# An expert stage re-cut from 24 tiles of two 64-token blocks to 31 tiles of one 128-token block

## The reference

```
normed = (x * rsqrt(mean(x*x) + 1e-6)) * ln_w
probs = softmax(normed @ w_router)              # 16 experts
expert_idx = argmax(probs)
keep = onehot * (cumsum(onehot, axis=1) <= 64)  # at most 64 tokens of a sequence for one expert
h = relu(expert_in @ wi[e])                     # 192 -> 768
expert_out = h @ wo[e]                          # 768 -> 192
next = where(routed, combined, normed)
return x + max(probs) * next
```

## Time and profile before

| | us |
|---|---|
| median of 3 runs | 405.36 |
| lowest, highest | 401.0, 406.44 |
| the profiled execution, whole | 408.49 |
| its span, first to last instruction | 406.8 |
| PE busy in the span | 320.6 (79%) |
| DVE busy | 262.2 (64%) |
| POOL busy | 203.8 (50%) |
| ACT busy | 191.6 (47%) |

### The profile page before, as it was taken

One profiled execution on the slowest core, in us unless ns is written; L12 is line 12 of the kernel. 1 busy time (PEld: TensorE's weight loads), 2 busy tenths in 40 slices (PEclk: granted clock), 3 DMA queues, 4 the chain that ended last, 5 costly groups with the idle time before them and its releaser, 6 DMA issues.

```text
span 406.8 us, 9205 instructions
## 1 busy us (share of the span) xinstructions
PE 320.6 (79%) x3246; PEld 234.4 (58%) x3246; DVE 262.2 (64%) x743; ACT 191.6 (47%) x405; POOL 203.8 (50%) x250
## 2 busy tenths in 40 slices
PE   0058798989889888998987803389999999999990
PEld 0056657769677676977867602345556666555560
DVE  7467846887878788767485636846656565556620
ACT  0613644967768687763844612033333333333320
POOL 5767650552553626401001446577666666755420
PEclk9999967998989899896998965599999999999997
DMA  5328820126152352703208951139311221111100
GB/s 138 89 63 222 244 60 1 21 60 176 33 161 72 96 146 48 203 1 99 75 9 246 291 154 39 39 105 293 107 46 51 60 58 54 48 46 53 48 3 0
DMA packets 33589, 38.22 MB, mean 94 GB/s; under 512 B 6480, under 2 KB 30777, under 8 KB 33556
## 3 DMA queue, kind: packets, MB, share of 16 engines
q1 hardware_dynamic: 25940, 24.58, 21.3%
q0 software_dynamic: 7040, 12.63, 12.5%
q10 hardware_dynamic: 576, 0.59, 0.4%
HBM read 31.36 MB, written 7.21 MB: 95 GB/s over the span
## 4 chain that ended last, share of the span: by engine, by line
PE 58%; POOL 11%; ACT 10%; issue 8%; DVE 7%; DMA 3%; POOLq 0%; ACTq 0%; SPq 0%; DVEq 0%
PE psum L1363 11%; PE psum L1140 7%; PE psum L1342 7%; PE psum L1141 7%; POOL weights L396 6%; PE psum L1347 4%; PE psum L1354 3%; PE psum L1258 3%; ACT shared L574 3%; PE psum L1175 3%; PE psum L1210 2%; POOL blk_token L458 2%; ACT L574 2%; PE psum L1134 2%; DMA token_rows<-shared 2%
## 5 line engine op out<-in xcount | busy, mean ns | idle before, releaser
L1087 DVE COPY shared<-weights 128x1152 f32 x96 | 69.1, 763 | 10.6 <-issue 10.5
L1258 PE MATMUL psum<-ident 128*128 128x128 f32 x200 | 34.0, 334 | 38.1 <-DMA qk_norm<-in_qk_norm 24.5
L473 POOL DMA_INDIRECT tower_out<-shared,oidx x24 | 37.1, 1547 | 38.6 <-DVE shared L1101 38.0
L1258 PEld LDWEIGHTS psum<-ident 128*128 128x128 f32 x200 | 32.6, 247 | 39.2 <-issue 24.5
L1363 PE MATMUL psum<-shared 128*64 128x192 f32 x576 | 52.1, 330 | 0.9 <-ACT shared L672 0.9
L404 POOL TENSOR_TENSOR small<-small,eps_of 128x2 f32<-128x2 f32 x32 | 6.8, 212 | 89.7 <-DVE small L768 66.2
L1363 PEld LDWEIGHTS psum<-shared 128*64 128x64 f32 x576 | 39.2, 137 | 19.4 <-issue 13.8
L1101 DVE SCALAR_TENSOR_TENSOR shared<-psum,shared 128x192 f32<-128x192 f32 x24 | 10.0, 418 | 46.0 <-PE psum L1363 46.0
L1140 PE MATMUL psum<-shared,weights 96*128 96x192 f32 (+1 forms) x96 | 36.2, 464 | 0.8 <-ACT weights L527 0.7
L1342 PE MATMUL psum<-shared 128*64 128x384 f32 x192 | 36.3, 499 | 0.5 <-ACT shared L664 0.5
L668 ACT ACTIVATE shared<-psum 128x768 f32<-128x768 f32 x24 | 19.5, 811 | 36.4 <-PE psum L1347 36.4
(11 more groups left out here) (179 smaller groups left out, 704.2 us busy)
## 6 DMA issues: line engine op xcount, KB each, us to landing
weights<-in_wo SPq DMA_DIRECT2D x16, 576.0 KB, 7.2
weights<-in_wi SPq DMA_DIRECT2D x32, 192.0 KB, 5.2
weights<-in_wi SPq DMA_DIRECT2D x32, 96.0 KB, 5.5
token_rows<-shared SPq DMA_DIRECT2D x14, 192.5 KB, 2.8
tower_out<-shared SPq DMA_DIRECT2D x14, 96.0 KB, 2.3
vectors<-in_vectors SPq DMA_DIRECT2D x1, 672.0 KB, 4.7
token_rows<-shared ACTq DMA_DIRECT2D x2, 192.5 KB, 2.8
blk_token<-expert_lists,blk_entry POOLq DMA_INDIRECT x24, 2.7
```

Source lines behind the costliest of these rows:

```text
L473: G.indirect_dma_start(out=out, out_offset=bass.IndirectOffsetOnAxis(ap=oidx[q % 2][:, :], axis=0), in_=res[q % 2], in_offset=None, bounds ...
L1087: V.tensor_copy(w_now[q % 2][k][:, lo:hi], weights[:, bass.ds(at[k] + lo, hi - lo)]).then_inc(sem(("wi_now", "wo_now")[part]), 1)
L1258: T.matmul(dst, ident[:, :], ident[:, 0:width], start=True, stop=True)
```

## The change

`BT` becomes 128. A block is now a whole tile of one expert, so each product of a tile is made once, for 128 tokens. 2,048 tokens over 16 experts need, beside the first block of each expert, at most 15 further blocks: 16 + 15 = 31 tiles. The first 16 tiles are fixed: tile q is the first block of expert q, PE reads its weights where they lie (`w_of`) and its tokens are column q of the list table. The other 15 are planned as before, with one `w_now` buffer each for odd and even. The whole list table, 64 KB, is read into `list_sb` by one transfer of SP once all lists are written; DVE then copies the column that a planned tile needs (`take_tokens`). `grow` has six buffers, and five tiles are gathered ahead.

```diff
-BT = P // 2
+BT = P
...
-NBLK = NSEQ * P // BT + NE
-NTILE = NBLK // 2
+NLATE = NSEQ * P // BT - 1
+NTILE = NE + NLATE
+NGROW = 6
...
+        def tokens_of(q):
+            return list_sb[:, q:q + 1] if q < NE else blk_token[:, q - NE:q - NE + 1]
...
-            sp.wait_ge(sem("p_logit"), NSEQ)
+            sp.wait_ge(sem("listed"), 16 * NSEQ)
+            load("lists_read", list_sb, lists.rearrange("(p q) o -> p (q o)", p=P))
             for u in range(3):
                 sp.wait_ge(sem(f"rows{u}"), 16)
...
-            list_tile(0)
-            list_tile(1)
             pool.wait_ge(sem("out_plain"), 32 * (NSEQ - 2))
             pool.wait_ge(sem("rows_last"), 32)
-            gather_rows(0)
-            list_tile(2)
-            gather_rows(1)
-            list_tile(3)
-            gather_rows(2)
-            for q in range(4, 8):
-                list_tile(q)
+            pool.wait_ge(sem("lists_read"), 16)
+            for q in range(NGROW - 1):
+                gather_rows(q)
             pool.wait_ge(sem("out_last"), 32)
             for q in range(NTILE):
-                if q + 3 < NTILE:
-                    gather_rows(q + 3)
-                if q + 8 < NTILE:
-                    list_tile(q + 8)
+                if q + NGROW - 1 < NTILE:
+                    gather_rows(q + NGROW - 1)
                 scatter(q)
...
+            unrouted(NPAIR - 1)
             steps = [0]
...
+            def take_tokens(j):
+                dve.wait_ge(sem("lists_read"), 16)
+                col = dve.value_load(blk_list[0:1, j:j + 1], min_val=0, max_val=NLISTS - 1)
+                V.tensor_copy(blk_token[:, j:j + 1], list_sb[:, bass.ds(col, 1)]).then_inc(sem("blk_token"), 1)
...
             for q in range(NTILE):
-                if q + 1 < NTILE:
-                    at = columns(q + 1)
-                    take_weights(q + 1, 0)
+                late_next = NE <= q + 1 < NTILE
+                if late_next:
...
+                    at = dve.value_load(blk_col[0:1, q + 1 - NE:q + 2 - NE], min_val=0, max_val=(NE - 1) * WCOL)
+                    take_weights(q + 1, 0)
                 if q >= 1:
                     result(q - 1)
-                if q + 1 < NTILE:
+                if late_next:
                     take_weights(q + 1, 1)
+                if 1 <= q <= NLATE:
+                    take_tokens(q - 1)
...
+            def w_of(q):
+                return w_by_expert[:, q, :] if q < NE else w_now[q % 2]
...
                 for b in range(2):
-                    for k in range(2):
-                        T.matmul(hid_ps[k * BT:(k + 1) * BT, b, :], gT[:, b * P + k * BT:b * P + (k + 1) * BT],
-                                 w_now[q % 2][k][:, b * WI2:(b + 1) * WI2], start=True, stop=False)
+                    T.matmul(hid_ps[:, b, :], gT[:, b * P:(b + 1) * P], w[:, b * WI2:(b + 1) * WI2], start=True, stop=False)
                 for b in range(2):
-                    for k in range(2):
-                        at = (1 - b) * P + k * BT
-                        last = T.matmul(hid_ps[k * BT:(k + 1) * BT, b, :], gT[REST[b], at:at + BT],
-                                        w_now[q % 2][k][REST[b], FF:WI_COLS], start=False, stop=True)
+                    last = T.matmul(hid_ps[:, b, :], gT[REST[b], (1 - b) * P:(2 - b) * P], w[REST[b], FF:WI_COLS],
+                                    start=False, stop=True)
...
                 for c in range(FC):
-                    for k in range(2):
-                        last = T.matmul(psum[q % 2][k * BT:(k + 1) * BT, 3, 0:D], hidT[:, c * P + k * BT:c * P + (k + 1) * BT],
-                                        w_now[q % 2][k][:, WI_COLS + c * D:WI_COLS + (c + 1) * D], start=c == 0, stop=c == FC - 1)
+                    last = T.matmul(psum[q % 2][:, 3, 0:D], hidT[:, c * P:(c + 1) * P],
+                                    w[:, WI_COLS + c * D:WI_COLS + (c + 1) * D], start=c == 0, stop=c == FC - 1)
```

More of the change, by code:

```diff
@@ L450, in _, with gather_rows @@
             phase_a(pool, 4, turn_pair)
-            pool.wait_ge(sem("listed"), 16 * NSEQ)
-            def list_tile(q):
-                pool.wait_ge(sem("blk_entry"), 1)
+            def gather_rows(q):
+                if q >= NE:
+                    pool.wait_ge(sem("blk_token"), q - NE + 1)
                 G.indirect_dma_start(
[L459 to L469, removed]
+                    out=grow[q % NGROW], out_offset=None, in_=rows,
+                    in_offset=bass.IndirectOffsetOnAxis(ap=tokens_of(q), axis=0),
+                ).then_inc(sem(f"rows{q % NGROW}"), 16)
             def scatter(q):
@@ L734, in _ @@
             dve.wait_ge(sem("ident"), 7)
[L735 to L738, removed]
             def reduce_args(i):
@@ L1047, in _, with total_over @@
             dve.wait_ge(sem("total"), len(BATCHES))
-            dve.wait_ge(sem("halves"), 3)
-            big, big2 = (shared[:, 4608 + 512 * k:4608 + 512 * k + NTILE * NE].rearrange("p (j e) -> p j e", e=NE) for k in range(2))
+            def total_over(v):
+                return v.unsqueeze(1).broadcast_to([P, NLATE, NE])
+            V.tensor_scalar(blk_pen[:, 0:NE], total[:, :], token_iota[:, 0:1], BIG, ALU.is_le, ALU.mult).then_inc(sem("first_pen"), 1)
             nb, cum, ones = (cols(plan, a, NE) for a in (16, 32, 48))
[L1052 to L1056, removed]
+            nth, ej, before, within, length, late = (cols(plan, 112 + 32 * a, NLATE) for a in range(6))
             planned(V.memset(ones, 1.0))
-            planned(V.scalar_tensor_tensor(over_k, total[:, :].unsqueeze(2).broadcast_to([P, NE, SPLIT]), BT + 0.5,
-                                           list_edge[:, :].unsqueeze(1).broadcast_to([P, NE, SPLIT]), ALU.add, ALU.is_gt))
+            planned(V.tensor_tensor(over_k, total[:, :].unsqueeze(2).broadcast_to([P, NE, SPLIT]),
+                                    list_edge[:, :].unsqueeze(1).broadcast_to([P, NE, SPLIT]), ALU.is_gt))
             planned(V.tensor_reduce(nb, over_k, AX, ALU.add))
@@ L1075, in _ @@
-            planned(V.tensor_scalar(late, half_pos[:, 0:1].broadcast_to([P, NTILE]), float(NLISTS), None, ALU.mult))
-            V.tensor_tensor(blk_entry[:, :], length, late, ALU.add).then_inc(sem("blk_entry"), 1)
-            unrouted(NPAIR - 1)
-            def take_weights(q, part):
-                lo, hi = ((0, WI_COLS), (WI_COLS, WCOL))[part]
-                if q >= 2:
-                    dve.wait_ge(sem(("b_hid", "b_y")[part]), q - 1)
-                for e in range(max(2 * q, ARENA_FIRST), min(2 * q + 2, NE)):
-                    dve.wait_ge(sem(f"weights{e}"), 80)
-                for k in range(2):
-                    V.tensor_copy(w_now[q % 2][k][:, lo:hi], weights[:, bass.ds(at[k] + lo, hi - lo)]).then_inc(
-                        sem(("wi_now", "wo_now")[part]), 1)
@@ L1104, in _ @@
-            dve.wait_ge(sem("blk_entry"), 1)
-            dve.wait_ge(sem("weights"), 80 * ARENA_FIRST)
-            at = columns(0)
-            take_weights(0, 0)
-            planned(V.tensor_tensor(big, over(expert_iota[:, :]), ej.unsqueeze(2).broadcast_to([P, NTILE, NE]), ALU.is_equal))
-            planned(V.tensor_tensor(big2, big, over(total[:, :]), ALU.mult))
+            planned(V.tensor_tensor(big, total_over(expert_iota[:, :]), ej.unsqueeze(2).broadcast_to([P, NLATE, NE]), ALU.is_equal))
```

104 lines of the change are left out of this document (62 added, 42 removed).

## The result

The changed kernel takes 441.03 us (median of 4 runs, 437.18 to 443.56) where the kernel before took 403.92 (4 runs, 401.0 to 406.44): 1.0895 times as long, 95% interval 1.0816 to 1.0973. Forecast was 433.5, range 426 to 441; the median lies at the very end of that range, 0.03 us past it. The direction and the mechanism are as forecast; the rise of 37.1 us is 9 us larger than the forecast 28.2. The profiled executions differ by 34.0 us in span: 440.8 against 406.8. The profiled execution of before (408.49) lies above all its timed runs, so this pair shows 3 us less than the medians do.

The account below looks back on a forecast made before the run. PE was taken to bound the expert stage: 29 steps of 5.08 us for 22 of 5.37 gave plus 28.8 us, the beginning minus 0.6, together 28.2 on the median 405.36. Forecast 433.5 us, range 426 to 441.

Parts of the forecast that it names:

- What bounds the kernel, and what a product costs: Expert stage: PE is the bound; a full-height product costs 0.32 us against 0.35 for a half-height pair, so little is saved.
- The rival by which the price goes with the records: Expert stage: twelve output records would take 1.05 us, POOL's 3.4 us a tile would rule, total 381 us; chance 3%.
- The two 64-row products side by side: Left-over products at L1341 overlap and take 0.65 us; rival without overlap: 1.30 us, total 453.5; chance 6%.
- a step of up to 5.3: Expert stage: case where shape changes all stay, PE's step 5.3 us a tile and the total 440 us.
- a first gather near 260.6: Start of expert stage: sign of being right, first gather at 260.6 where it stood at 261.17, a gain of 0.6 us.
- a first hidden product within 2 us of 266: Start of expert stage: sign of being right, PE's first hidden product within 2 us of 266 in the timeline.
- the signs for being wrong: Step below 4.8 or above 5.3 us, PE waiting for DVE or a gather in the last 15 tiles, first tile after 268.
- PE's step: Each tile: transposes 0.88, hidden 1.30, left-over 0.65, output 1.95, two shape changes 0.30, together 5.08 us for 5.37.
- The beginning: Before the first gather: plan and two list fetches go, a 64 KB read comes; minus 0.6 us, ends minus 3.4 and plus 2.3.
- The late tiles: Last 15 tiles run without waits; rival stall of 1.5 us a tile, plus 22 us, 455; chance 3%.
- the 0.4 us of longer steps near the start: Early expert stage: 0.4 us above 22 x 5.37 in the kernel before, forecast to stay after the change.
- 0.3 off the last tile for two changes of shape: Last hidden product to the end: 8.3 us before, forecast 8.0 with two changes of shape fewer.

Follow-up runs that it names:

- e2: Kernel before with the products of every tile's second block left out: step 5.35 us for 5.37, one timed execution 404.19 us.
- e6: Changed kernel with the left-over channels' products (64 rows by 128 columns) left out, result wrong: step 4.19 us, one timed execution 421.07 us.
- e9: Changed kernel with the left-over product ahead of the main hidden product: step 5.157 us as median of all tiles, one timed execution 437.79 us.
- e4: Kernel before with the left-over product ahead of the main hidden product: step 5.22 us, 402.05 against 406.12 us, ratio 0.9941.
- e1: Changed kernel with its last seven tiles (24 to 30) left out: 402.84 us against 406.12 for the kernel before, ratio 0.986.
- e3: Changed kernel with each full-height product issued as two half-height ones with the same weights: step 5.37 us, one run 440.81 us.
- e5: Changed kernel with PE's filler begun when the last tokens are placed, 26 filler products instead of 10: 460.42 us, 1.0674 times the kernel before.
- e10: Kernel before with the left-over product first and POOL's first gather ahead of the second list fetch: 403.15 against 404.28 us, ratio 0.9948.
- e11: Kernel before with the left-over product first and tile 3's gather ahead of the list fetches of tiles 4 to 7: 428.48 against 432.97 us, ratio 0.9876.
- e7: Kernel before with left-over product first, list table read at once (DVE taking three tiles' tokens) and early PE filler: 426.5 against 432.19 us, ratio 0.9923.

## Why the prediction was right, and where its sizes were off

**What bounds the kernel, and what a product costs: right.** The twelve output products in pairs at 0.35 and the full-height ones at 0.32 were read from the profile of before, and e2 shows it directly: the second product of each pair costs next to nothing. The rival by which the price goes with the records was out at the first look: twelve records took 2.06 us, not 1.05.

**The two 64-row products side by side: right.** L1341 is 0.84 with its change of shape; one after the other it would have been 1.4.

**The range held only just.** The median of 441.03 is at the end of 426 to 441. The width stood there for a step of up to 5.3, which was to give 440; the step was 5.23, which by the forecast's own sum gives 438, and 3 us came from elsewhere. Three of the signs that the forecast named for being right were missed: a step of 5.0 to 5.15 us, a first gather near 260.6 (258.45) and a first hidden product within 2 us of 266 (263.41). The others came: no gaps, the output products in 2.06 us, the pair at L1341 in 0.84, one step before and after tile 16. None of the signs for being wrong came.

**PE's step: right in kind, mis-sized, 5.08 for 5.23.** This is the term that matters: 0.15 x 29 = 4.4 us of the 5.8 that are missing. I put 0.15 on each change of shape. In the rows the 0.15 has two parts: a change behind a group, 0.09 to 0.10, and a head of the next group. The head is 0.05 for the half-height products and 0.10 for the full-height ones (the output product: 2.10 - 1.95 - 0.10 before, 2.06 - 1.95 after), and the full-height hidden product shows 0.07 behind the transposes. Four changes cost 0.6 before; two now cost 0.4, and the head behind the transposes 0.07. Transposes 0.87 + hidden 0.07 + 1.29 + 0.10 + left-over 0.10 + 0.65 + 0.09 + output 0.10 + 1.95 = 5.22. This account gave 4.2 for e6 and 5.15 for e9 before they ran, and 4.19 and 5.157 came.

That the head is the first weight load of the group, which nothing hides, is argued from its size and not shown by itself: no run varied the load alone. It goes with the length of the load's record rather than with the columns loaded. The loads of the half-height products (64 columns) take 0.13 to 0.14 us and those of the full-height ones (128 columns) 0.19; those of the transposes load 128 columns in 0.14, and behind a change of shape their head is 0.05 (L1334 to L1335 is 0.16 us in the kernel before; L1326 to L1327, with no change ahead, is 0.11 in the changed one). So in the trace of before every head in the step was 0.05; it showed that the price has two parts, but not the 0.10.

The Trainium skill's rule in "TensorEngine Tiling (Array Packing)", "Key Properties", that switching the mode drains the array, agrees with the time that e4, e6 and e9 show at each change. That section gives no size, so nothing there could confirm the forecast's 0.15.

**The beginning: too small a gain, then a cost that I had not listed.** I kept the list writes as what holds the first fetch and took 0.6 us. In the changed kernel they had landed 2.3 us after the last issue (SP's read goes out at 255.93). In the kernel before the first fetch went out 3.8 after it, so there the plan did hold it, and 2.1 us came free. In the profiled execution the clock took 1.8 of that back. Where it had risen in time (e1, e3) the first step is 4.03 and 4.05, so this cost was not in every execution.

**The late tiles: right.** No wait in the last 15, the same 5.231 step.

**The end: unexplained.** 1.7 us more from the last result to the end of the span. It is 11.6 to 11.7 in all six profiles of the changed kernel and its variants with 31 tiles, 10.55 in the one with 24 (e1), and 9.6 to 9.9 in the kernel before and its variants, with 24 as well. So about 1.1 goes with the tile count and 0.7 with something else in the changed kernel; what either is was not tried.

**Two small terms.** The forecast let the 0.4 us of longer steps near the start stay, and they did not recur; so the 29 steps are 3.9 us above the forecast in the table and not 4.4. It took 0.3 off the last tile for two changes of shape, and nothing came off.

## What to carry to other kernels

Products that fill the array by sitting side by side in it are already paid: making one full product of two half ones saves their records, not their time, so compare tile counts before record counts. Here 24 tiles of 5.37 beat 31 of 5.23, and the tile count is the worst case over the data. Order the groups so that as few neighbours as can be differ in array shape, and read the price of a change at the head and the tail of a group, not as a mean. A head that was read from one form of product need not hold for another. And when a start is pulled forward, look at what the clock does there, in more than one profile.

## What was not expected of the hardware

- A group behind a change of shape has a head of 0.05 us where its weight loads take 0.13 to 0.14 and of 0.10 where they take 0.19, on top of 0.09 to 0.10 for the change behind the group before it.
- A second half-height product beside the first costs 0.03 us in a whole tile of twenty (e2: 5.35 for 5.37).
- PE idle for 3.2 us behind 8 us of filler, and the granted clock fell back within that gap and stayed low for 10 us (e5). It also fell just behind an idle time of 3.05 us (e10), and not over one of 2.65 (e11).
- With the same ten filler products the granted clock was up by the first hidden product in four profiles (e1, e3, e6, e9) and not in a fifth (the changed kernel).
- DVE stood idle for 0.8 to 0.9 us ahead of most copies whose column comes from a register loaded from a table (e7).
